# Attention over node batches: where in a step TensorE reads the node tiles of the next destinations

## The reference, cut to what matters

```
def _gat_layer(x, src, dst, W, a_src, a_dst, b, heads, concat):
    h = (x @ W).reshape(n, heads, -1)
    al_s = jnp.einsum('nhf,hf->nh', h, a_src)
    al_d = jnp.einsum('nhf,hf->nh', h, a_dst)
    e = jax.nn.leaky_relu(al_s[src] + al_d[dst], NEG_SLOPE)
    m = jax.lax.stop_gradient(jax.ops.segment_max(e, dst, num_segments=n))
    ex = jnp.exp(e - m[dst])
    denom = jax.ops.segment_sum(ex, dst, num_segments=n)
    alpha = ex / (denom[dst] + 1e-16)
    out = jax.ops.segment_sum(h[src] * alpha[:, :, None], dst, num_segments=n)
    ...
h = _gat_layer(h, src, dst, W1, att_src1, att_dst1, b1, HEADS, True)
...
out = _gat_layer(h, src, dst, W2, att_src2, att_dst2, b2, 1, False)
```

## Time and profile before

| | |
|---|---|
| three timed executions | 7345.85 to 7351.69 us, median 7349.14 |
| span of the profiled execution | 7337.7 us, 11.4 less than the median |
| mean granted TensorE clock | 0.770 |
| TensorE products and transposes | 4785.5 us busy, 65% |
| VectorE | 4350.1 us busy, 59% |
| ScalarE | 2618.8 us busy, 36% |
| GpSimd | 3686.7 us busy, 50% |

### The profile page before, as it was taken

The page is one execution under the profiler, slowest core; times in us unless marked ns, Lnnn a source line. Parts: engine busy times, 40 slices in busy tenths (PEclk is TensorE's granted clock), DMA queues, the critical chain, the costliest instruction groups (busy, mean ns, idle before and its releaser), DMA issues. The chain is left out here.

```text
span 7337.7 us, 99573 instructions
## 1 busy us (share of the span) xinstructions
PE 4785.5 (65%) x21954; PEld 3537.1 (48%) x21954; DVE 4350.1 (59%) x12539; ACT 2618.8 (36%) x7524; POOL 3686.7 (50%) x3680
## 2 busy tenths in 40 slices
PE   5666699996556666666565667466666666666662
PEld 4544588885444444444444445344444444444442
DVE  8999776665555555555555558545454544545457
ACT  6774222221444444444444445222222222222221
POOL 2332311112566666666666653566666666666660
PEclk8788899997777776777777779667777777777776
DMA  8999634333344444344444434333333333333336
GB/s 330 392 391 385 257 122 135 111 111 96 109 116 112 116 112 115 112 115 112 116 111 116 112 104 125 113 111 105 112 108 111 113 106 111 105 111 106 111 112 225
DMA packets 384886, 1062.90 MB, mean 145 GB/s; under 512 B 103714, under 2 KB 195798, under 8 KB 359654
## 3 DMA queue, kind: packets, MB, share of 16 engines
q0 software_dynamic: 168928, 459.50, 23.6%
q1 hardware_dynamic: 205782, 548.21, 20.6%
q10 hardware_dynamic: 9904, 52.57, 1.8%
HBM read 795.11 MB, written 264.87 MB: 144 GB/s over the span
## 5 line engine op out<-in xcount | busy, mean ns | idle before, releaser
L259 POOL DMA_INDIRECT rows<-table_d,idx x3328 | 3237.8, 973 | 2034.5 <-issue 780.7
L307 PE MATMUL pG<-rows,onehot 128*128 128x264 f32 (+1 forms) x6656 | 2497.6, 527 | 892.3 <-issue 531.0
L510 DVE TENSOR_TENSOR acc<-acc,pG 128x264 f32 (+1 forms) x3328 | 1414.3, 425 | 1797.8 <-remote 691.7
L307 PEld LDWEIGHTS pG<-rows,onehot 128*128 128x128 f32 x6656 | 1609.0, 260 | 1436.0 <-issue 837.5
L371 ACT ACTIVATE onehot<-pQ 128x1024 f32<-128x1024 f32 (+1 forms) x512 | 440.1, 859 | 2506.1 <-DMA g2b<-in_g_b 1530.2
L378 ACT ACTIVATE rows<-rows 128x64 f32<-128x64 f32 (+1 forms) x4480 | 1255.2, 367 | 16.9 <-issue 12.5
L946 PE MATMUL pH<-hT_pre,w1h 128*128 128x256 f32 x1568 | 468.7, 464 | 191.6 <-ACT hT_pre L808 152.1
L946 PEld LDWEIGHTS pH<-hT_pre,w1h 128*128 128x128 f32 x1568 | 363.2, 238 | 281.1 <-ACT hT_pre L808 169.7
L1109 DVE SCALAR_TENSOR_TENSOR run<-run,same_e,ea 128x96 f32<-128x96 f32 x1567 | 484.3, 309 | 3.0 <-DMA ea<-in_ea 1.2
L1109 DVE SCALAR_TENSOR_TENSOR run<-run,cut_e,ea 128x96 f32<-128x96 f32 x1567 | 484.0, 309 | 0.0
L492 DVE TENSOR_TENSOR rows<-rows,pA 128x1024 f32<-128x1024 f32 x384 | 466.7, 1215 | 4.4
(11 more groups left out here) (295 smaller groups left out, 4555.5 us busy)
## 6 DMA issues: line engine op xcount, KB each, us to landing
rows_d<-run SPq DMA_DIRECT2D x97, 1536.0 KB
onehotT<-drow_d SPq DMA_DIRECT2D x128, 832.0 KB
ea<-in_ea SPq DMA_DIRECT2D x98, 768.0 KB
rows<-table_d,idx POOLq DMA_INDIRECT x3328
pre_d<-pre ACTq DMA_DIRECT2D x49, 1024.0 KB
pre_in<-pre_d SPq DMA_DIRECT2D x49, 1024.0 KB, 5.1
hrow_c<-table_d SPq DMA_DIRECT2D x98, 256.0 KB
tab<-tab_d SPq DMA_DIRECT2D x64, 260.0 KB
```

The lines of the kernel that those rows point to most:

```text
L259: g.indirect_dma_start(out=rows[:, at.par, k, 0:XF + H], out_offset=None, in_=table, in_offset=bass.IndirectOffsetOnAxis(ap=idx[:, at.par, ...
L307: mm = pe.matmul(pG[(k + 2 * at.par) % 4][:, 0:W], onehot[:, k, :], rows[:, at.par, k, :], start=True, stop=True)
L510: v.tensor_tensor(to, to, pG[(k + 2 * at.par) % 4][:, 0:W], ALU.add).then_inc(added, 1)
```

## The change

In `step`, TensorE's `tiles = node_tiles_of(m)` moves from the head of the step, ahead of the products of items 12 to 15, to the middle of the softmax chain, behind the transposes L328 and L329. Nothing is added or removed, and the other engines' code is the same, row for row.

```
@@ -315,8 +315,6 @@
                 if not chain:
                     part(EARLY, TB)
                     return
-                if ahead:
-                    tiles = node_tiles_of(m)
                 part(EARLY, 16)
                 spans(n, 0, first)
                 pe.wait_ge(z_ready, n.n + 1)
@@ -327,6 +325,8 @@
                 pe.sem_inc(pe_passed, 1)
                 pe.transpose(psE[:, 0:HT], loc[:, 0:1], keep["ident"][0:HT, 0:HT])
                 pe.transpose(psE[:, HT:2 * HT], loc[:, P - 1:P], keep["ident"][0:HT, 0:HT]).then_inc(edge_ready, 1)
+                if ahead:
+                    tiles = node_tiles_of(m)
                 spans(n, 1)
                 part(18, 20)
                 pe.wait_ge(cd_ready, n.n + 1)
```

## The result

The changed kernel takes 7795.83 us (median of four executions, 7791.31 to 7801.94), the kernel before 7348.38 in the runs beside it (7345.85 to 7351.69). The ratio is 1.0614, 95% interval 1.0599 to 1.0629: 447 us slower. The profiled execution has a span of 7800.2 us against 7337.7, so 462 more.

What follows compares the result with a forecast made beforehand. The attentions were taken as bound by waits around a ring, about 40 us a step. 527 us paid in mid-chain, less 0 at the head and 227 given back, made 300 us more: 7650 us, range 7430 to 7880.

Steps and rivals of the forecast that it cites:

- The load at the head is hidden: Head of the step: late signal of items 14 and 15 covers the load, so removing it there gains 0.
- check 1: Gap of 5.44 us ahead of items 12 to 15 gone, sums of 14 and 15 still 20.0 us behind first gather.
- the late signal: TensorE's signal for items 14 and 15, seen 4.9 or 9.4 us late, when GpSimd's unbroken gather run ends.
- The load in mid-chain is paid in full: Behind L329, no spare time: 395.5 us for odd batches and 131.4 for even, together 527 us.
- check 2: L326 to L334 takes 2.96 + 6.2 us in steps of odd batches, 2.96 + 2.1 in the others.
- check 3: GpSimd pauses ahead of item 18's gather; `scale` follows L343 within a microsecond instead of 2.9.
- What is given back: Behind L334, signals become prompt: 1.8 us a step, 227 us in all, between 0 and 3.7 a step.
- second stretch of late signals: Behind L334: `scale` and the weights' copy wait for "remote", 4.84 and 3.32 us, which the delay can fill.
- Check 4: Period of a long step grows by some 4.4 us, of a short one by 0.3.
- slower still: GpSimd's 8 gathers of items 18 to 25 delay the weights' transposes signal: 248 us on top of 527, 8124; chance 0.09.
- Faster: Head of the step is the bound: 3.39 us gained in each of 64 steps, 217 us, 7193; chance 0.12.
- The same: Load as hidden in mid-chain as at the head, needing 4.18 us a step given back: 7349; chance 0.05.

Runs made afterwards that it cites:

- The second group: Runs on a chip whose traces show no late signals; the kernel before took 6442.16 us there.
- the aligned halves: Kernel before with each half of the node-tile list padded from 26 to 32 numbers: 6381.9 us against 6442.16, ratio 0.9907.
- a second load: Kernel before with two really issued register loads at the head of the step: 6800.8 us against 6442.16, ratio 1.0563.
- The pause ahead of item 22: Changed kernel with GpSimd waiting ahead of item 22's gather until items 0 to 21 have landed: 7847.67 us, ratio 1.0622.
- the first and third groups: Runs on chips with late signals; the kernel before took 7392.88 us in one and 7388.52 in the other.

## Why the prediction was right, and the term that was mis-sized

**The load at the head is hidden: right, within 33 us.** With the load gone from the head, the sums of items 14 and 15 still stand 20 us behind the first gather in the changed kernel (check 1), and in the kernel without any load they keep their place in the step. The 33 us include what the destinations gained by fixed registers. The second group adds a condition: the cover goes with the late signal, and where a chip has none the load at the head costs time: 23% of the 260 us that the aligned halves save, and 69% of a second load.

**The load in mid-chain is paid in full: right.** L326 to L334 grew by 6.3 and 2.4 us against 6.2 and 2.1 (check 2), and taking 260 us of load away gave 219 to 248 back. Ahead of L328 the load costs 131 us and behind L329 447, and the spare 4.1 us fit with rows' ends that come only 1.4 to 2.1 us later there.

**GpSimd's pause and the prompt `scale`: right** (check 3). It pauses 3.18 and 7.13 us ahead of item 18, and `scale` follows within 0.04 us.

**What is given back: mis-sized.** The prediction said 1.8 us a step, 227 us, in the second stretch of late signals. Up to the weights it happened nearly so: the steps are later there by 0.4 and 4.1 us in the second attention, 0.4 and 4.3 in the first, where the forecast for the whole step had 0.3 and 4.4. Taken over 62 even and 64 odd steps that is 62 x 0.4 + 64 x 4.2 = 294 us, my 300. Then most of what was given back is taken again: at the next batch's first product the steps are later by 1.6 and 7.1, and 0.6 and 5.9. The difference, 1.2, 3.0, 0.2 and 1.6 us, over 31 or 32 steps of each kind, is 37 + 96 + 6 + 51 = 190 us. 294 + 190 = 484, against 462 in the spans. Of the 227 us some 65 were left (527 - 462). Check 4, which was about the period of the steps, failed by it: the long steps grew by 6.9 us in the second attention and 5.9 in the first where 4.4 was forecast, the short ones by 1.5 and 0.6 where it was 0.3.

The step that failed is the place where the gain was booked. The prediction counted it at the end of the last sums and took the next batch to follow. The next batch's first product needs two things, the weights and the end of TensorE's own destinations. Before, the weights were late by their own late signal (3.32 us of "remote" ahead of ScalarE's copy), and TensorE made the destinations meanwhile; the weights came last, and the first product followed them by 1.4 to 2 us. Making that signal prompt helps the weights: from L334 they come 1.7 to 2.4 us sooner. TensorE's own way from L334 to the destinations shrinks by about 1.5 us in the second attention and grows by about 0.5 in the first (table). In the changed kernel the first product follows the first weights by 3.5 to 4.5 us in the odd steps, because the destinations end last.

What makes them end so late is a slow stretch in the destinations. The load delays the gather of item 18, and the eight gathers of items 18 to 25 then follow without a pause, from 6037.64 to 6047.37. TensorE's instructions become slow at 6044.03, 6.4 us into that run, and the last slow one is at 6047.61. The pause ahead of item 22 shows that this run is the cause: it takes the slow stretch away. The stretch is not all new. The destinations' line in the profile page, its idle time after the second bar, in the kernel before and in the changed one:

```profile
L287 PE MATMUL pS<-adt,onehotT 128*128 x3328 | 322.4, 175 | 139.3 <-issue 123.8
```

```profile
L287 PE MATMUL pS<-adt,onehotT 128*128 x3328 | 291.5, 172 | 285.1 <-issue 272.4
```

The idle time was 139.3 us before and is 285.1. In the first attention the destinations take as long as before (table); there the loss is that they start later and no longer lie in the shadow of the weights. So the rival *slower still* had the right run, but the wrong victim. It put the lateness on the signal of the weights' transposes and at 248 us on top of 527; it fell on the destinations, and the time from the weights to the next batch cost 190 us inside the 527.

**Faster: fell.** Its price was VectorE's idle 3.39 us in each odd step; the kernel without a load gave at most 38 us in all, not 217. **The same: fell.** It needed 4.18 us a step given back; 0.5 came.

**The price of a register.** The Trainium skill, "Runtime: NRT & Kernel Launch", section on instruction fetch mechanics, gives about 200 ns a register. The same page of the Trainium skill says in its terms that TENSOR_LOAD loads registers from HBM, while the list here stands in a tile of the kernel in SBUF (`jrow_pe`), so the figure was not made for this load. The aligned load shows 2106/26 = 81 ns from byte 128, as from byte 0; from byte 104 it is 6.18 us, 238 ns a register. In these traces it depends on where the list begins.

**What stays open.** Why a chip's sequencers are slow while GpSimd gathers, and why one of the chips is not, no trace here shows. On that chip GpSimd gathers with even fewer pauses than on the others, so an unbroken run alone does not make a signal late. TensorE's granted clock was also higher there in the kernel before, 0.82 against 0.75 in the first and third groups; whether that is a cause or a consequence is not shown. Nor was it shown that start alignment alone, and not some other property of byte 104, makes the load long: bytes 0 and 128 were short, 104 long, and nothing else was tried.

## What to carry to other kernels

A gap on the timeline is worth what the next link gains when it closes, and here a gap of 5.44 us was worth at most half a microsecond a step and the same instruction 6 to 7 us where the chain was tight. When a late link becomes prompt, ask what was done in its shadow: that work is the next bound. When a delay moves work of an engine (GpSimd's gathers), follow it to where it lands next, one stage further than the place where the gain is booked. And when a cover is a property of the chip rather than of the program, measure on more than one chip before building on it.

## What the runs showed of the hardware that I had not expected

- **Chips differ in it.** The same kernel took 7348, 7393 and 7389 us in three groups of runs and 6442 in a fourth. The slow ones show register instructions of up to 1.4 us (median 0.046) on TensorE, in the changed kernel while GpSimd gathers; the fast one shows none over 0.052 among the 3328 of each trace.
- **The late signals go with the gathers' run.** They come to light about 2 us behind the end of its last gather (1.9 us in the kernel before, 5632.74 to 5634.68), also where the run is ended by a pause put in by hand (2.07 us).
- **A register load's time depends on where it begins.** 26 registers take 2.1 us from byte 0 or 128 and 6.2 from byte 104, and it is the place and not the batch's parity: odd batches were short too once their half began at byte 128.
- **An unused register load is dropped by the compiler**, so doubling a suspected cost has to use both results.
